# Four graph blocks on one core: the low half of a turned row split one step earlier in blocks 1 and 2, the normed rows of block 3 made on ScalarE

## The reference

```python
def _layernorm(x, axis=-1, eps=1e-05):
    m = jnp.mean(x, axis=axis, keepdims=True)
    v = jnp.var(x, axis=axis, keepdims=True)
    return (x - m) / jnp.sqrt(v + eps)
...
x = _layernorm(x + _L0_gnn_ref(x, adj, L0_gnn_W_stack), axis=-1)   # two attention layers: softmax(Wh Ws^T) * adj @ Wh
x = _layernorm(x + _L1_gnn_ref(x, adj, L1_gnn_W), axis=-1)         # relu((A + I, scaled by degree) @ x @ W)
x = _layernorm(x + _L2_gnn_ref(x, adj, ...), axis=-1)              # relu(mean of neighbours @ Wn^T + x @ Ws^T + biases)
x = _layernorm(x + _L3_gnn_ref(x, adj, ...), axis=-1)              # adj @ (relu(adj @ (x @ W1) + b1) @ W2) + b2
```

## Time and profile before

| | before |
|---|---|
| time, median of 3 runs (lowest to highest) | 748.05 us (747.47 to 749.39) |
| time of the profiled execution | 747.91 us |
| its span, first to last instruction | 746.1 us |
| PE busy | 719.9 us (96%) |
| DVE busy | 481.4 us (65%) |
| ACT busy | 338.8 us (45%) |
| POOL busy | 324.6 us (44%) |
| chain that ended last, by engine | PE 86%, DVE 8%, issue 2%, ACT 2%, POOL 1% |
| block 1's first to block 2's first sum step on VectorE | 508.3 us to 604.4 us |
| block 2's first sum step to block 3a's | 604.4 us to 678.8 us |
| block 3b, first residual to the last normed rows | 712.4 us to 743.3 us |

### The profile page before, as it was taken

One profiled execution on the slowest core, in us unless ns is written; L12 is line 12 of the kernel. 1 busy time (PEld: TensorE's weight loads), 2 busy tenths in 40 slices (PEclk: granted clock), 3 DMA queues, 4 the chain that ended last, 5 costly groups with the idle time before them and its releaser, 6 DMA issues.

```text
span 746.1 us, 13241 instructions
## 1 busy us (share of the span) xinstructions
PE 719.9 (96%) x3984; PEld 611.2 (82%) x3984; DVE 481.4 (65%) x1111; ACT 338.8 (45%) x785; POOL 324.6 (44%) x346
## 2 busy tenths in 40 slices
PE   8999999999999999999999999999979998899996
PEld 7888888888888888888888888887757777679985
DVE  3867777777776656566566566555666657775466
ACT  5666665656666463556546547522222412221112
POOL 1057676767766315553644544456562000003200
PEclk9999999999999999999999999999999999999999
DMA  7133324242331301822323323376652211110012
GB/s 267 36 135 118 137 85 169 85 148 105 114 139 57 127 0 65 205 72 92 120 70 99 112 70 118 67 142 147 154 136 64 89 59 58 58 42 3 1 44 73
DMA packets 63139, 72.39 MB, mean 97 GB/s; under 512 B 36336, under 2 KB 56432, under 8 KB 58992
## 3 DMA queue, kind: packets, MB, share of 16 engines
q1 hardware_dynamic: 63088, 71.78, 31.0%
HBM read 46.60 MB, written 16.78 MB: 85 GB/s over the span
## 4 chain that ended last, share of the span: by engine, by line
PE 86%; DVE 8%; issue 2%; ACT 2%; POOL 1%; DMA 0%; SPq 0%; DVEq 0%; ACTq 0%; POOLq 0%
PE scores L1902 38%; PE ob L1902 26%; PE tb L1902 8%; PE tb L2071 7%; PE xb L1902 3%; DVE zb L1611 1%; DVE xt_l L1222 1%; DVE zb L1678 1%; DVE zb L1614 1%; DVE norm_values L1684 1%; PE tb L2015 1%; DMA xres<-features_scratch 0%; PE xb L2096 0%; PE tb L1921 0%; PE xb L1950 0%
## 5 line engine op out<-in xcount | busy, mean ns | idle before, releaser
L671 POOL TENSOR_TENSOR prob<-prob,arow 128x512 f32<-128x512 f32 x128 | 191.9, 1521 | 146.4 <-ACT prob L875 146.4
L1902 PE MATMUL ob<-val,stationary 128*128 128x512 f32 x960 | 186.7, 344 | 0.0
L1902 PEld LDWEIGHTS ob<-val,stationary 128*128 128x128 f32 x960 | 146.7, 189 | 18.4
L1222 DVE TENSOR_TENSOR stationary<-tb,stationary 128x512 fp32r<-128x512 f32 x128 | 85.5, 688 | 57.2 <-ACT stationary L776 56.1
L1902 PE MATMUL scores<-wst_h,whs_h 128*128 128x512 f32 x256 | 102.6, 401 | 0.0
L1902 PE MATMUL scores<-wst_h,whs_l 128*128 128x512 f32 x256 | 100.0, 390 | 0.0
L1902 PE MATMUL scores<-wst_l,whs_h 128*128 128x512 f32 x256 | 99.8, 390 | 0.0
L1319 DVE TENSOR_REDUCE row_values<-scores 128x1 f32<-128x512 f32 x128 | 86.0, 683 | 13.5 <-PE scores L1902 12.0
L776 ACT ACTIVATE stationary<-tb 128x512 fp32r<-128x512 f32 x128 | 72.9, 595 | 42.4 <-PE tb L2071 40.9
L875 ACT ACTIVATE prob<-scores,row_values 128x512 f32<-128x512 f32 x128 | 86.8, 690 | 11.4 <-DVE row_values L1326 11.4
L2071 PE MATMUL tb<-ident,prob 128*128 128x128 f32 x512 | 71.7, 272 | 0.0
(11 more groups left out here) (227 smaller groups left out, 1203.2 us busy)
## 6 DMA issues: line engine op xcount, KB each, us to landing
arow<-in_adj SPq DMA_DIRECT2D x32, 1024.0 KB, 5.2
adjacency_halves<-arow SPq DMA_DIRECT2D x16, 512.0 KB, 3.0
features_scratch<-xs SPq DMA_DIRECT2D x32, 128.0 KB, 1.9
xres<-features_scratch SPq DMA_DIRECT2D x32, 128.0 KB, 2.1
keep<-in_x SPq DMA_DIRECT2D x4, 512.0 KB, 6.6
xres<-in_x SPq DMA_DIRECT2D x16, 128.0 KB, 2.1
self_term_scratch<-rst SPq DMA_DIRECT2D x16, 128.0 KB, 1.7
rin<-self_term_scratch SPq DMA_DIRECT2D x16, 128.0 KB, 2.1
```

Of the source, the lines that this page charges most:

```text
L671: nc.gpsimd.tensor_tensor(prob[u][:, cs], prob[u][:, cs], arow[u][:, cs], ALU.mult).then_inc(g.msk.sem, 1)
L1222: return nc.vector.tensor_tensor(dst, v, h.bitcast(F32), ALU.subtract)
L1902: return nc.tensor.matmul(o, l, r, start=start, stop=stop)
```

## The change

In blocks 1 and 2 `rows_lo` of tile s-2 moves ahead of `residual` of tile s-1 in VectorE's slot. In block 3b VectorE no longer writes the normed rows. It makes a shift per row, minus the mean times the inverse deviation, into `nmax`, once the normed rows of two tiles back are done; ScalarE makes the normed rows by an Identity activation with the inverse deviation as scale and the shift as bias, each behind the deviation of the next tile. The waits for the buffers of the result move to ScalarE with it.

```diff
--- before.py
+++ after.py
@@ -375,6 +375,7 @@
         s_emov = sem("block3_moving_ready")
         s_fh = sem("block3_sums_hi")
         s_fl = sem("block3_sums_lo")
+        s_shift = sem("block3_shift_ready")
         s_kb = sem("block3_residual_biased")
 
         def attention_bank(b, u):
@@ -1094,6 +1095,19 @@
                 act.wait_ge(F.done, q + 1)
                 copy(fsum_h[:, first * P:stop * P], fbank[q][:, 0:(stop - first) * P]).then_inc(s_fh, 1)
 
+            def normed(t):
+
+                u = t % 2
+                act.wait_ge(s_shift, t + 1)
+                if t < 2:
+                    ge(act, C.out[u], 8 * NT)
+                    ge(act, C.xtr, NT)
+                elif t < 4:
+                    ge(act, Dg.y, NT)
+                ge(act, F.out[t % 4], 16 * (t // 4))
+                nc.scalar.activation(finished[t % 4][:, :], zb[u][:, :], ACT.Identity, bias=nmax[u][:, :],
+                                     scale=rstd[:, u:u + 1]).then_inc(F.new.sem, 1)
+
             def general():
 
                 with act.Fori(0, NT) as q:
@@ -1171,6 +1185,9 @@
                             if t in LEAD:
                                 sums_hi(LEAD.index(t))
                             deviation(t // 2 * 2, t % 2)
+                            if t:
+                                normed(t - 1)
+                        normed(NT - 1)
                         continue
                     if a is E:
                         for t in range(NT):
@@ -1711,14 +1728,9 @@
                         return
                     if quick and a is F:
 
-                        if t < 2:
-                            ge(dve, C.out[u], 8 * NT)
-                            ge(dve, C.xtr, NT)
-                        elif t < 4:
-                            ge(dve, Dg.y, NT)
-                        ge(dve, a.out[t % 4], 16 * (t // 4))
-                        nc.vector.tensor_scalar(finished[t % 4][:, :], zb[u][:, :], mv[:, u, 0:1], rstd[:, u:u + 1],
-                                                ALU.subtract, ALU.mult).then_inc(a.new.sem, 1)
+                        ge(dve, a.new, t - 1)
+                        nc.vector.scalar_tensor_tensor(nmax[u][:, :], mv[:, u, 0:1], -1.0, rstd[:, u:u + 1],
+                                                       ALU.mult, ALU.mult).then_inc(s_shift, 1)
                         return
                     rows_free(b, u)
                     if a.proj and not a.last:
@@ -1824,11 +1836,10 @@
                         p, pp = before(b, u), before(b, u, 2)
                         if ep:
                             total(*p)
-                        if ep:
-                            residual(*p)
                         if fin:
                             rows_lo(*pp)
                         if ep:
+                            residual(*p)
                             norm(*p)
                         if fin:
                             self_term(*pp)
```

## The result

| | before | after |
|---|---|---|
| time, median of 12 runs each (lowest to highest) | 748.62 us (747.47 to 749.41) | 746.2 us (745.26 to 746.67) |
| ratio after to before, 95% interval | | 0.9967 (0.9958 to 0.9976) |
| time of the profiled execution, its span | 747.91, 746.1 us | 746.33, 744.5 us |
| first residual of block 3b | 712.37 us | 702.51 us |
| end of the last normed row | 743.30 us | 742.25 us |

The kernel is 2.4 us faster; 745.15 was forecast. The two middle lines say why it is no more: the work ahead of block 3b ends 9.86 us earlier, and the stretch from there to the last normed row, 30.93 us before, takes 39.74 us. The two changes nearly cancel out.

What follows compares the result with a forecast made beforehand. TensorE, busy 96%, was bounded by its waits for VectorE's low half (the split) in blocks 1 and 2, and VectorE's loop in block 3b. 10.5 us gained less 7.6 lost gives 2.9: median 745.15 us, range 742.0 to 749.3.

Steps and rivals of the forecast that it cites:

- Block 1, 7.6 predicted: Split moved ahead in block 1: 1.5 us at projection 0, 5.3 at projections 3 to 9, 0.8 at 9 to 13.
- The doubled tiles: Block 1, tiles with doubled written-out steps: VectorE's loop per step falls from 5.26 to 4.1 us, in two of six steps.
- the four other steps: Block 1, projections 3 to 9: steps set by TensorE's own work, 4.4 us, 4.5 each with the hand-over.
- 0.4 us over for SP: Block 1: allowance for SP's transfers and self-term store, raising projections 3 to 9 from 26.2 to 26.6 us.
- the first rival: Blocks 1 and 2: SP's store chain and later normed rows halve the split's gain to 6.3 us; 749.3 us, chance 0.21.
- Block 2, 2.9 predicted: Split moved ahead in block 2: VectorE's 3.9 us slots give 2.4 us in projections 3 to 9, neighbouring steps 0.5.
- waits for turned rows in place of the split: Sign against the prediction: TensorE waiting for turned rows where it had waited for the split; no size given.
- Block 3b, 7.6 predicted: Normed rows on ScalarE in block 3b cost 7.6 us: tile 15's residual 7.3 later, the end 0.3 more.
- The loop: Block 3b: residual waits for ScalarE's normed row of two tiles back, 2.12 us per tile against 1.33.
- Half a first part: The first rival: block 1 gains 4.8 us, block 2 1.5, less 7.6 in block 3b; 749.3 us, chance 0.21.
- ScalarE's turn longer: Block 3b rival: ScalarE's turn exceeds 0.79 us, perhaps by table loads; over 0.3% slower from 0.35 us more; chance 0.12.
- The loop not binding: Block 3b rival: VectorE runs freely beside ScalarE, the part costs at most 0.3 us; 737.9 us, chance 0.06.

Runs made afterwards that it cites:

- With two buffers: Split moved ahead in blocks 1 and 2 only, with two self-term buffers in block 1, against the kernel before: 738.0 us, again 737.74 us.
- the four-buffer kernel: Changed kernel with four buffers instead of two for block 3b's residual rows and per-row values: 740.45 us, 5.75 us under the changed kernel.

## Why the prediction came out as it did

**Block 1, 7.6 predicted, 6.85 in the trace, 7.1 alone.** Projection 0's wait went (1.38 us of the 1.5), and projections 9 to 13 take 21.24 us, 21.3 predicted. The doubled tiles run in 4.07 and 4.25 us (projections 4 to 5 and 7 to 8), 4.1 predicted, so the loop was cut as read. The term mis-sized is the four other steps: 4.54, 5.03, 4.69 and 4.79 us, where I had 4.5 each and 0.4 us over for SP; so projections 3 to 9 came out at 27.37 us, outside the 26 to 27 that the prediction named as its sign. The 5.03 is the step with the 0.71 us wait for the store, the first rival's own mechanism. With two buffers and no such wait the four are 4.56, 4.79, 4.54 and 4.80: the two right behind a doubled tile stay long. In these two the turning step starts 1.16 or 1.17 us after the chunk ahead of it, 0.92 or 0.93 in the other two, right behind the normed rows (541.47 and 541.53 in the rows above). That is the rival's other half, a turning step that waits for later normed rows, and it is over half of the 0.4 us by which they exceed the 4.4 of TensorE's own work.

**Block 2, 2.9 predicted, 3.0 in the trace (9.86 less 6.85), 3.4 alone.** Projections 3 to 9 take 23.59 us, 23.4 predicted; VectorE's slots in and between the doubled tiles lie 3.90 us apart, once 4.00, against the 3.9 that was read off the last written-out tile. The prediction named waits for turned rows in place of the split as a sign against it. They came, 2.0 us, and the gain came all the same: VectorE's slot sets the length of these steps, so TensorE waits in one place or the other.

**Block 3b, 7.6 predicted, 8.8 in the stretch, 7.7 alone.** The loop, its place and its closing wait were right. Two terms of it were short. Residual to deviation is 1.29 us and not 1.25; what adds the 0.04 is not shown, for in the changed kernel it is 1.26 in tile 0, without a shift between statistics and mean, and 1.26 in tile 1 too, with one. ScalarE to VectorE is 0.13 us and not 0.08. The normed row itself, which no row of before showed, is 587 ns against 0.59. Loop: 2.21 instead of 2.12; by the prediction's own 1.5 us for each 0.1, that is 1.3 us more, and 7.6 + 1.3 = 8.9. Part of that agreement is luck. Tile 8's residual comes 20.52 us after the first, 19.9 predicted, and tile 15's 37.13, 35.9 predicted; in the kernel with block 3b's part alone tile 15's comes after 36.88, so the loop's two terms are worth about 1.0. The other 0.25 lies in the two steps around tile 8 (3.94 and 2.35 us, 3.82 and 2.21 in that kernel), where TensorE's granted clock was lower (last section). From the end of the last row to the end of the span it takes 2.25 us, 2.8 before, which gives 0.55 back. Nothing in the edit explains that; the stretch is 2.25 to 3.4 us long in the kernels of this study.

**The sum.** In the two profiles 9.86 gained, 8.81 lost, 0.55 back: 1.6 us, the difference of the spans. The prediction had 10.5 less 7.6. The gain was 6% under the forecast and the loss in the stretch 16% over it; that the difference still came out near, 2.9 forecast and 2.4 found between the medians, is partly luck: in the two profiles it is 1.6, and that with the 0.55 at the end. In the prediction's bounds 747.9 less 12 plus 6.2 is 742.1, not 742.2; nothing hangs on it.

**The rivals.** Half a first part: no, though its store and its later normed rows showed. ScalarE's turn longer: the loop is 0.09 us longer where 0.35 was the point of decision, and there is no table load. The loop not binding: no; the four-buffer kernel shows that case, and even then the part costs 1 to 2 us (1.8 in the stretch; 1.3 between the medians 740.45 and 739.15, whose intervals overlap), not 0.3.

## What to carry to other kernels

Before work moves to an engine with time to spare, follow its output buffer: with two buffers and a consumer that stands behind the next tile's result on another engine, the loop per tile is the sum over both engines (2.21 us here against 1.33), whatever their busy shares say. Give such a hand-over a third and fourth buffer, or put the consumer ahead of the wait in its queue; either gave back 5.75 us here. And where a written-out loop waits for one step, move that step ahead of everything that doesn't need to precede it: that move alone was worth 9.4 us.

## What the runs showed of the hardware

**A residual that doubles beside GpSimd.** In these rows the instruction that starts second takes longer. GpSimd's addition in the changed kernel:

```profile
538.38 0.73 POOL L752 TENSOR_TENSOR rin<-pm 128x256 f32<-128x256 f32 x1 [1.29 <-DVE zb L1631]
```

and in the kernel before, where the residual had begun 0.14 us earlier (535.08):

```profile
535.22 0.88 POOL L751 TENSOR_TENSOR rin<-pm 128x256 f32<-128x256 f32 x1 [2.15 <-DVE zb L1614]
```

Second, the addition takes 0.88 us instead of 0.74; first, it makes the residual take 0.94. A residual that starts 0.40 us into the addition takes 0.62 (561.76 and 561.36); in both cases it ends 0.28 or 0.29 us behind the addition's end. The Trainium skill, SBUF — State Buffer, section "Who interferes with whom", says that a VectorE instruction with two inputs in SBUF contends with a GpSimd instruction that reads SBUF; the trace agrees, with the numbers above.

**A lower granted clock in block 3b.** There TensorE now waits for the copies of the sums, 1.30 us ahead of 721.70 and 2.05 us ahead of 734.90; before, its one such wait was 0.5 us. The changed kernel by stretches of 5 us (busy times, then the granted clock):

```profile
core 0: us, PE busy (x) PEld busy (x) DVE busy (x) ACT busy (x) POOL busy (x), PEclk, DMA share, GB/s
...
720.00:725.00 5.00, 3.48 (x18) 3.08 (x17) 2.04 (x8) 1.95 (x5) 0.00 (x0) 0.75 0.12 41
725.00:730.00 5.00, 4.93 (x39) 4.72 (x37) 2.29 (x11) 1.95 (x6) 0.00 (x0) 0.91 0.16 52
```

Part of these stretches ran at the lower level, 1.2 GHz. TensorE's timeline there:

```profile
721.70 0.39 PE L1913 MATMUL scores<-w3bh,fsum_h 128*128 128x256 f32 x1 [1.30 <-ACT fsum_h L777]
...
724.45 0.41 PE L1913 MATMUL scores<-w3bh,fsum_h 128*128 128x256 f32 x1
724.66 0.41 PE L1913 MATMUL scores<-w3bl,fsum_h 128*128 128x256 f32 x1
...
726.42 0.28 PE L1913 MATMUL scores<-w3bh,fsum_h 128*128 128x256 f32 x1
726.54 0.28 PE L1913 MATMUL scores<-w3bl,fsum_h 128*128 128x256 f32 x1
```

Projections of 256 columns start 0.21 us apart at the lower level and 0.12 at the upper, 2.4 GHz. Tile 9's residual follows tile 8's after 2.35 us instead of 2.21. The kernel with block 3b's part alone kept a granted clock of 1.00 from 715 to 745 us, though its TensorE waited the same 1.30 us, ahead of 731.84; so what made the clock fall here is open. Its residual of tile 8 came 20.40 us after the first, against 20.52, and that of tile 15 36.88, against 37.13: the lower clock cost about 0.25 us.
